# Layer 0 of a four-layer image kernel: one group of scores matmuls for both token halves, and a new order of the pipelined step

## The reference

```
x  = _ln(x, n1g, n1b); if shifted: roll by (-4, -4)
q, k, v = x @ qkvw.T + qkvb           # per window of 64 tokens
attn = softmax(q * SCALE @ k.T + rpb[RPI] (+ MASK if shifted))
x  = shortcut + (attn @ v) @ pw.T + pb
x  = x + gelu(_ln(x) @ f1w.T + f1b) @ f2w.T + f2b
```

## Time and profile before

| | before |
|---|---|
| runs | 974.94, 970.7, 974.59 us, median 974.59 |
| profiled execution | 970.56 us, its span 968.2 us |
| busy PE / DVE / ACT / POOL | 796.0 / 798.8 / 574.5 / 231.4 us |
| mean granted TensorE clock | 0.871 |
| first and last `xa` (`affine_a`) | 11.3 and 563.8 us |
| last addition of layer 0 | 605.6 us |

### The profile page before, as it was taken

One profiled execution on the slowest core, in us unless ns is written; L12 is line 12 of the kernel. 1 busy time (PEld: TensorE's weight loads), 2 busy tenths in 40 slices (PEclk: granted clock), 3 DMA queues, 4 the chain that ended last, 5 costly groups with the idle time before them and its releaser, 6 DMA issues.

```text
span 968.2 us, 20293 instructions
## 1 busy us (share of the span) xinstructions
PE 796.0 (82%) x7926; PEld 526.2 (54%) x7926; DVE 798.8 (83%) x2011; ACT 574.5 (59%) x857; POOL 231.4 (24%) x270
## 2 busy tenths in 40 slices
PE   3799999999999999999999988889587866533346
PEld 1577877787788777777777765365121111100013
DVE  8788889888888998888899985665619999899974
ACT  1376777777777677777776664133547664655133
POOL 6222222222222222222222221293201221222101
PEclk9799999999999999999999997979685765565667
DMA  8100000000000000002000000100001665667501
GB/s 236 60 1 3 1 2 2 2 1 2 2 2 2 2 2 2 2 1 105 1 3 2 2 1 2 49 1 1 1 1 34 131 131 98 120 122 137 111 0 33
DMA packets 11621, 34.11 MB, mean 35 GB/s; under 512 B 1880, under 2 KB 4360, under 8 KB 11272
## 3 DMA queue, kind: packets, MB, share of 16 engines
q0 software_dynamic: 5904, 21.24, 11.5%
q1 hardware_dynamic: 5623, 11.60, 4.0%
HBM read 10.81 MB, written 0.79 MB: 12 GB/s over the span
## 4 chain that ended last, share of the span: by engine, by line
PE 62%; DVE 27%; ACT 5%; issue 3%; DMA 1%; POOL 1%; POOLq 0%; SPq 0%; DVEq 0%; ACTq 0%
PE narrow L1458 6%; PE wide L1381 4%; PE scores_a L1430 4%; PE scores_b L1430 4%; DVE prod L982 4%; PE last L1535 4%; DVE prod L990 3%; PE scores_b L1441 3%; PE scores_a L1417 3%; PE scores_b L1417 3%; PE scores_a L1441 3%; PE narrow L1488 3%; PE last L1531 2%; PE wide L1521 2%; PE last L1508 2%
## 5 line engine op out<-in xcount | busy, mean ns | idle before, releaser
L379 POOL TENSOR_TENSOR stb<-stb,neg_half 128x4 f32<-128x4 f32 x48 | 48.3, 1006 | 252.4 <-DVE stb L674 252.4
L1108 ACT ACTIVATE d<-d 128x768 f32<-128x768 f32 x96 | 80.6, 839 | 18.4 <-DVE d L621 17.9
L1458 PEld LDWEIGHTS narrow<-v,pt 128*64 128x64 f32 x2304 | 79.8, 139 | 13.4 <-issue 13.4
L1458 PE MATMUL narrow<-v,pt 128*64 128x54 f32 x2304 | 86.0, 226 | 0.1
L1705 PE MATMUL scores_b<-xb,gates_w 128*32 128x512 bf16 x192 | 26.9, 576 | 59.5 <-DVE yo L1002 51.5
L374 POOL TENSOR_TENSOR sta<-sta,neg_half 128x4 f32<-128x4 f32 x48 | 48.8, 1016 | 104.5 <-DVE sta L561 104.5
L1115 ACT ACTIVATE pt<-scores_a 128x768 f32<-128x768 f32 x48 | 38.8, 809 | 56.6 <-PE scores_a L1441 56.6
L1124 ACT ACT_TABLE_LOAD x47 | 60.3, 1283 | 0.8
L1108 ACT ACT_TABLE_LOAD x46 | 59.0, 1283 | 0.8
L608 DVE TENSOR_REDUCE mx<-scores_a 128x12 f32<-128x768 f32 x48 | 46.0, 958 | 15.8 <-PE scores_a L1430 15.8
L1124 ACT ACTIVATE ga<-wide 128x512 f32<-128x512 f32 x48 | 28.7, 598 | 49.6 <-PE wide L1521 49.6
(11 more groups left out here) (347 smaller groups left out, 2184.9 us busy)
## 6 DMA issues: line engine op xcount, KB each, us to landing
gsum<-mag POOLq DMA_DIRECT2D x14, 512.0 KB, 4.6
ysum<-yo POOLq DMA_DIRECT2D x7, 768.0 KB, 5.6
ysum<-xd POOLq DMA_DIRECT2D x6, 768.0 KB, 5.8
gsum<-mag POOLq DMA_DIRECT2D x14, 256.0 KB, 4.7
wts<-in_wpack SPq DMA_DIRECT2D x6, 442.0 KB, 6.5
sed_w<-in_sed_in SPq DMA_DIRECT2D x1, 2304.0 KB, 8.1
graw<-in_gates_in SPq DMA_DIRECT2D x1, 1152.0 KB, 5.0
x_all<-in_x_tok SPq DMA_DIRECT2D x8, 96.0 KB, 2.7
```

Source lines behind the costliest of these rows:

```text
L1108: act.activation(d, d, ACT.Exp).then_inc(p_ready[u], 1)
L1458: op = pe.matmul(y_ps[64 * b:64 * b + 64, q * VO:(q + 1) * VO], t.pt[:, q, h, 64 * b:64 * b + 64], t.v[:, q, b, h * VO:(h + 1) * VO], star ...
```

## The change

PE, `scores`: the two calls `scores(n, 0)` and `scores(n, 1)`, which stood in two places of the step, are one call `scores(n)` with u as the innermost loop, so that consecutive matmuls go to the four row groups in turn (partitions 0, 32, 64, 96). One semaphore `pe_S` takes the place of two. `maxima` of both halves wait for it.

All four loops are written in a new order, and chunks are further apart: PE's loop has one step more (`SLOTS + 4`), ACT's one more, DVE's and POOL's two more. GELU is split into `gelu_a` and `gelu_b`, called in different places for different chunks. `windows_T`, `project_v`, `values` and `transpose_z` wait for another reader of `narrow`, as the new order of its six uses asks. On DVE `table_rest` goes from k % 8 == 2 to 4, `centre` from 4 to 5, `table_low` from 5 to 7; the sign multiplications of layer 1's weights from steps 40 to 47 to steps 42 to 49, the final statistics and fills two steps later. ACT's `table_high` and `table_middle` keep their steps (1 and 4). No instruction is added or left out.

```diff
@@ -397,16 +397,16 @@
-            for k in range(SLOTS + 4):
-                if k >= 45:
-                    rstd_f(k - 45)
-                rstd_b(k - 3)
-                add_b2(k - 3)
+            for k in range(SLOTS + 6):
+                if k >= 47:
+                    rstd_f(k - 47)
+                add_b2(k - 5)
                 rstd_a(k)
                 if k == 0:
                     rstd_e(1)
                     set_values()
                     rstd_e(2)
+                rstd_b(k - 4)
                 if k == 1:
                     pool.memset(ypad[:], 0.0).then_inc(set_ypad, 1)
             rstd_f(7)
...
@@ -735,68 +734,69 @@
-            for k in range(SLOTS + 4):
-                if k >= 45:
-                    final_stats(k - 45)
-                if k == 51:
+            for k in range(SLOTS + 6):
+                if k >= 47:
...
-                invert(k - 3)
-                divide(k - 3)
-                subtract(k - 2, 0, 1)
-                take_o(k - 3)
                 if k == 1:
-                    embed_centre(1)
-                normal_a(k - 1)
-                if k == 1:
+                    normal_a(0)
                     embed_square(1)
                     embed_centre(2)
                     embed_square(2)
-                add_proj(k - 3)
-                squares_b(k - 3)
-                variance_b(k - 3)
-                maxima(k - 2, 1)
-                subtract(k - 2, 1, 0)
-                subtract(k - 2, 1, 1)
-                normal_b(k - 3)
-                if k == 50:
+                    embed_finish(1)
+                squares_a(k)
+                normal_b(k - 5)
+                variance_a(k)
+                if k > 1:
+                    normal_a(k - 1)
+                maxima(k - 3, 0)
+                subtract(k - 3, 0, 1)
+                subtract(k - 3, 0, 0)
+                maxima(k - 3, 1)
+                add_mlp(k - 6)
+                subtract(k - 3, 1, 1)
+                invert(k - 4)
+                divide(k - 4)
+                subtract(k - 3, 1, 0)
+                if k == 52:
                     fill(2)
                     fill(3)
-                if k == 2:
+                take_o(k - 4)
+                take_k(k - 2)
+                add_proj(k - 4)
+                squares_b(k - 4)
+                variance_b(k - 4)
+                if k == 3:
                     dve.wait_ge(set_v, 9)
                     dve.wait_ge(set_on, 6)
-                take_v(k - 2)
-                take_k(k - 1)
-                if k == 1:
-                    embed_finish(1)
-                squares_a(k)
-                variance_a(k)
-                add_mlp(k - 4)
-                maxima(k - 1, 0)
-                subtract(k - 1, 0, 0)
-                if 45 <= k < 51:
-                    final_normal(k - 45)
-                if 40 <= k < 48:
-                    if k == 40:
+                take_v(k - 3)
+                if k == 0:
+                    embed_centre(1)
+                if 47 <= k < 53:
+                    final_normal(k - 47)
+                if 42 <= k < 50:
...
                 if k == 2:
                     embed_finish(2)
                     centre(0)
+                if k % CHUNKS == 5 and k // CHUNKS < BLOCKS - 1:
+                    centre(k // CHUNKS + 1)
                 if k % CHUNKS == 4 and k // CHUNKS < BLOCKS - 1:
-                    centre(k // CHUNKS + 1)
-                if k % CHUNKS == 2 and k // CHUNKS < BLOCKS - 1:
                     table_rest(k // CHUNKS + 1)
-                if k % CHUNKS == 5 and k // CHUNKS < BLOCKS - 1:
+                if k % CHUNKS == 7 and k // CHUNKS < BLOCKS - 1:
                     table_low(k // CHUNKS + 1)
...
@@ -1152,27 +1158,29 @@
-            for k in range(SLOTS + 3):
+            for k in range(SLOTS + 4):
+                exponential(k - 2, 0)
+                take_q(k - 1)
+                exponential(k - 2, 1)
                 take_PT(k - 2, 0)
-                exponential(k - 2, 1)
-                take_q(k - 1)
-                affine_b(k - 3)
-                if k == 50:
-                    fill(3)
                 take_PT(k - 2, 1)
-                gelu(k - 3)
-                exponential(k - 1, 0)
+                gelu_b(k - 4)
                 affine_a(k)
                 if k % CHUNKS == 1 and k // CHUNKS < BLOCKS - 1:
                     table_high(k // CHUNKS + 1)
                 if k % CHUNKS == 4 and k // CHUNKS < BLOCKS - 1:
                     table_middle(k // CHUNKS + 1)
-                if k == 49:
+                affine_b(k - 3)
+                if k == 50:
                     for c in range(3):
                         fill(c)
+                gelu_a(k - 3)
                 if k == 50:
+                    fill(3)
...
@@ -1358,7 +1366,9 @@
                 pe.wait_ge(z1_ready, n + 1)
                 if n >= 2:
-                    pe.wait_ge(x1_ready, n - 1)
+                    pe.wait_ge(v_ready, n - 1)
+                elif n == 1:
+                    pe.wait_ge(xa_ready, 1)
...
@@ -1416,20 +1426,20 @@
-            def scores(n, u):
+            def scores(n):
                 if not live(n):
                     return
                 t = st[n % 2]
-                if u == 0:
-                    pe.wait_ge(q_ready, n + 1)
-                    pe.wait_ge(k_ready, n + 1)
+                pe.wait_ge(q_ready, n + 1)
+                pe.wait_ge(k_ready, n + 1)
                 for v in range(2):
                     for b in range(2):
                         for r in range(2):
-                            rows, cols = slice(64 * r + 32 * u, 64 * r + 32 * u + 24), slice(128 * v + 64 * b, 128 * v + 64 * b + 64)
-                            op = pe.matmul(sc_bank[u][64 * b:64 * b + 64, r, 192 * v:192 * v + 192], t.q[rows, cols], t.k[rows, :, cols],
-                                           start=False, stop=True, skip_group_check=True)
-                op.then_inc(pe_S[u], 1)
+                            for u in range(2):
+                                rows, cols = slice(64 * r + 32 * u, 64 * r + 32 * u + 24), slice(128 * v + 64 * b, 128 * v + 64 * b + 64)
+                                op = pe.matmul(sc_bank[u][64 * b:64 * b + 64, r, 192 * v:192 * v + 192], t.q[rows, cols], t.k[rows, :, cols],
+                                               start=False, stop=True, skip_group_check=True)
+                op.then_inc(pe_S, 1)
...
@@ -1493,7 +1505,9 @@
                 pe.wait_ge(z2_ready, n + 1)
-                if live(n + 1):
+                if live(n + 3):
+                    pe.wait_ge(xa_ready, n + 4)
+                elif live(n + 1):
...
@@ -1577,39 +1591,34 @@
-            for k in range(SLOTS + 3):
+            for k in range(SLOTS + 4):
+                project_qk(k - 1)
+                values_T(k - 3)
+                probs_T(k - 2, 0)
+                proj(k - 3)
+                probs_T(k - 2, 1)
+                fc1_b(k - 4)
+                project_v(k - 2)
+                bias(k - 1, 0)
                 bias(k - 1, 1)
-                proj(k - 2)
-                scores(k - 1, 1)
                 windows_T(k)
+                scores(k - 1)
+                transpose_z(k - 3)
+                if k == 51:
+                    final_T(4)
+                    final_T(5)
+                    conv(0, (2,))
+                fc2(k - 4)
                 if k == 50:
-                    conv(0, (2,))
-                fc2(k - 3)
-                if k == 49:
                     pe.wait_ge(set_ypad, 1)
                     pe.wait_ge(conv_ready, 1)
                     conv(0, (0,))
-                probs_T(k - 1, 0)
-                project_v(k - 1)
-                project_qk(k)
-                bias(k, 0)
-                transpose_z(k - 2)
-                probs_T(k - 1, 1)
-                scores(k, 0)
-                values(k - 1, 0)
-                values(k - 1, 1)
-                fc1_a(k - 2)
-                fc1_b(k - 2)
-                if k == 48:
-                    final_T(0)
-                    final_T(1)
-                values_T(k - 1)
-                if k == 48:
-                    final_T(2)
-                    final_T(3)
+                fc1_a(k - 3)
+                values(k - 2, 0)
+                values(k - 2, 1)
```

More of the change, by code:

```diff
@@ L1124, in gelu, with gelu_b @@
                     act.activation(t.g1[:], hid_bank[:, :, 0:256], ACT.Gelu).then_inc(g1_made, 1)
+            def gelu_b(n):
+                if live(n):
+                    t = st[n % 2]
                     act.wait_ge(pe_f1b, n + 1)
+                    if n >= 2:
+                        act.wait_ge(pe_f2, n - 1)
                     act.activation(t.g2[:], z_ps[:, 0:256], ACT.Gelu).then_inc(g2_made, 1)
@@ L1453, in values @@
                         pe.wait_ge(xb_in, n)
+                    else:
+                        pe.wait_ge(xa_ready, 3)
                 for v in range(2):
```

37 lines of the change are left out of this document (20 added, 17 removed).

## The result

| | before | after |
|---|---|---|
| median of the runs on one chip | 972.75 us (970.7 to 974.94) | 949.27 us (947.41 to 949.96) |
| profiled execution, span | 970.56, 968.2 us | 948.81, 946.7 us |
| busy PE / DVE / ACT / POOL | 796.0 / 798.8 / 574.5 / 231.4 | 765.9 / 799.2 / 575.0 / 236.0 us |
| `xa` of chunk 5, of chunk 47 | 80.3, 563.8 | 70.3, 527.7 |
| last addition of layer 0 | 605.6 + 0.35 | 582.3 + 0.35 |

The ratio is 0.977, with an interval of 0.974 to 0.979: 23 us faster. Predicted were 935 us, with a range of 925 to 958. Sign and main mechanism came out; the gain is 23 us where some 36 were expected, and the time lies in the part of the range that had been set up for rivals which did not occur.

A forecast was written before the change was run, and what follows sets the result against it. The prediction took the layer-0 loop to be bound by PE, with DVE close behind. From 970.56 us it took loop -31.5, fill -10 and drain +5 to 934, stated as 935, range 925 to 958 (own band 925 to 944).

The forecast's parts named there:

- Rival 1: Scores group on PE: eight passes do not run at once, group up to 1.47 us; 952 to 958 us; chance 0.20.
- rival 2: Layer-0 loop: DVE's waits stay, its in-order queue keeping 0.7 us per step; 955 us, or 966 if all stays; chance 0.12.
- Loop bound by PE, group of 32 passes at 0.81 us: Layer-0 loop: PE alone sets the plain step; the merged scores run eight passes at a time, 0.81 us, upper bound 1.47.
- The rule of about 25 ns: Scores group: matmul starts at least about 25 ns apart would make 32 passes 0.80 instead of 0.67 us, estimate 940.
- Plain step 10.4 (10.34 + 0.1): Layer-0 loop: PE's sum falls from 11.15 to 10.34 us, plus about 0.1 of exposed waits; 10.3 to 10.5.
- rival 3: Layer-0 loop: ACT's two table loads delay PE every step; at 1.2 us late the time is 985 us; chance 0.05.
- Tables 12, signs and final statistics 3: Layer-0 loop: moved table work exceeds DVE's slack, 12 us; sign multiplications and final statistics cost about 3 us on top.
- Loop 452: The 42 steps between `xa` of chunk 5 and the last: 42 x 10.4 + 12 + 3 = 452 us, against 483.5.
- Fill -10: Before `xa` of chunk 5: about 3.5 us less work in front and 6 to 7 less idle; -10, range 0 to -15.
- Drain "with the final work on DVE about 47: +5": Last `xa` to last MLP addition: 41.8 us becomes 43.9, about 47 with final work on DVE; +5, range 0 to +10.
- The 362 us behind stay: Everything after 606 us in the profile, behind layer 0's end: 362 us, unchanged.
- rival 4: Filling and draining: deeper ones lose the loop's gain, needing a drain of +25 or more; nothing much happens; chance 0.03.

## Why the prediction was right, and where it was off

- **The number**: 949.27 lies in the range of 925 to 958, but outside the forecast's own band of 925 to 944. The range went up to 958 for rivals 1 and 2, and neither occurred, so that the time fell inside is luck as far as the number goes. The sign and what makes the loop shorter are not luck. Of the marks set for being right, the start of the group (0.59 us from first to last), the plain step, PE's waits (11.1 us in 42 steps, 0.26 each) and the `xa` of chunk 5 came; DVE's share in the loop (93.6% for over 94%) and the last `xa` (527.7 for 522) were missed.
- **Loop bound by PE, group of 32 passes at 0.81 us**: right. The group is 0.84, eight at a time, so nearly the whole of the second group's 0.81 went away. Rival 1 (four at a time) is out. My reason for it, that the u innermost is what lets eight run, was wrong: with u outermost they run too.
- **The rule of about 25 ns** between starts, which I took from the Trainium skill, "TensorE: Matmul & The Clock Gate", section "Wait — 56ns, not 53.3ns?", and which would have given 940: it doesn't hold for passes on different row and column groups. 32 starts fit into 0.59 us, 19 ns apart on average, and eight into 0.05 us. "Part 3: Packing small matmuls — row/col tiling" of the same page gives about 4 ns between the starts of such tiles; the trace has 6 to 7 ns. I had written that the trace of the kernel before doesn't decide it, from the average of 37 ns. It does decide it, in a narrower window:

```profile
306.44 0.39 PE L1430 MATMUL scores_b<-k,q 24*64 24x192 f32 x4
```

Four passes are done in 0.39 us, of which one takes 0.37 (the 372 ns of the earlier trace rows), so their starts lie within 0.02 us. The average hid the pauses between the batches.

- **Plain step 10.4 (10.34 + 0.1)**: right; 10.45, of which all other work on PE took 0.08 more than before. The covers that I had worked out to 0.05 to 0.2 us held: no other engine is on the chain. Rivals 2 and 3 are out: DVE's idle time in the loop shrank from 54.1 to 29.4 us. What rival 2 describes was to be seen with the merged group in the old order.
- **Tables 12, signs and final statistics 3**: the table steps cost 12.9 over 10.47 each, the last six steps 4.8. The sum is near, but partly by another way: I had priced queue time alone, and 3 us of it are lower clock. The experiments added what I hadn't seen, that at their old steps the tables would have cost 39 us more.
- **Loop 452**: 457.4. The term that was small is the plain step (+2.9 over 42 steps, 10.47 for 10.4), then the last six steps (+1.8) and the tables (+0.9).
- **Fill -10**: the number is right, -10.0, its parts less so. DVE has 5.3 us less to do there (59.5 for 64.8) and 4.7 less idle, where I had 3.5 and 6 to 7. And the new order with two groups has a fill of 75.6: about 5 of the 10 us come with the merged group, which I had put at nothing here.
- **Drain "with the final work on DVE about 47: +5"**: this is the term that was mis-sized most: 54.6, +12.8, beyond the bound of +10. I counted four steps at 10.4 and added the final work as a sum, and didn't place it in the queues: it stands ahead of the last two `zb` on DVE, and the first convolution ahead of the last `fc1_a` on PE. PE's two waits for `zb` there are 2.50 and 4.76 us. That they come to 7.3 and the drain is 7.6 over my 47 proves nothing: with the end of layer 0 rearranged the drain is 47.8, though 4.5 us of those waits are still there, and with `fc1_a` alone ahead of the convolution and `zb` still late it was 55.2. That the order of the final work made the drain long is shown by the 47.8; how much each place in the queues cost isn't.
- **The 362 us behind stay**: about +1.8, of the size by which this unedited part differs between the profiles here (362 to 366 us).

By terms: loop +5.4, drain +7.8 (12.8 for 5), the rest +1.8, together 15.0 over the sum of 934; the profiled execution took 948.81. The mark that I had set for rival 4 (a drain of over 55 us) was nearly reached; its result, no gain, was not.

## What to carry to other kernels

Where small matmuls use part of the rows and columns, put all that can run side by side into one group without anything between: each separate group pays its whole length, here 0.8 us, and inside the group the order hardly matters. Such a merge asks for a new order of the consumers, so look at who used the first half while the second was made; done without that, in the one place tried, it cost 19% here. To see how many matmuls run side by side, look at a window of one batch; an average over the group hides it. And when a pipeline is made deeper, lay out the drain engine by engine, with each queue's order: the last chunks' critical stages go ahead of whatever follows, and long side work is cut into pieces of less than the slack of a step.

## What the hardware showed that I had not expected

- TensorE started four passes of `scores_b` 0.05 us behind the first four of `scores_a`, ahead of twelve passes that come first in the program.
- A wait of TensorE of 0.8 to 1.05 us in a loop that is otherwise full was followed by 3.4 us at the 1.2 GHz level in some cases (two of five such waits in each of two profiles of the same kernel, in different blocks; none of the five with u outermost), and each such stretch made its step about 1.5 us longer. Where waits were in every step, the mean clock of the loop was 0.83 and the loop grew by 172 us, though the work was the same.
